# Routing of the first half moved into the last steps of the attention, at two places of a four-layer kernel

## The reference

```python
    def _L0_xattn_ref(q, k, v, mask, Wq, Wk, Wv, Wo):
        qh = split_heads(q, Wq, Sq)
        kh = split_heads(k, Wk, Sk)
        vh = split_heads(v, Wv, Sk)
        scores = jnp.einsum('bhqd,bhkd->bhqk', qh, kh) / jnp.sqrt(jnp.asarray(D_K, qh.dtype))
        m = mask[:, None, :, :]
        scores = jnp.where(m == 0, jnp.asarray(-1000000000.0, scores.dtype), scores)
        p = jax.nn.softmax(scores, axis=-1)
        out = jnp.einsum('bhqk,bhkd->bhqd', p, vh)
        out = out.transpose(0, 2, 1, 3).reshape(B, Sq, H * D_K)
        return out @ Wo.T

    def _L0_ffn_ref(x, gate_w, fc_w, proj_w):
        gates = jax.nn.softmax(xt @ gate_w, axis=-1)
        top_v, top_i = jax.lax.top_k(gates, K)
        top_v = top_v / jnp.sum(top_v, axis=-1, keepdims=True)
        h = jnp.einsum('nd,edf->enf', xt, fc_w)
        h = jax.nn.gelu(h, approximate=False)
        eo = jnp.einsum('enf,efd->end', h, proj_w)
        ...
        out = jnp.sum(sel * top_v[:, :, None], axis=1)

    x = x + _L0_xattn_ref(_layernorm(x, axis=-1), ctx_1024, ctx_1024, mask_Bx1xS2_if1, ...)
    x = x + _L0_ffn_ref(_layernorm(x, axis=-1), L0_ffn_gate_w, L0_ffn_fc_w, L0_ffn_proj_w)
    ...
    x = x + _L3_xattn_ref(_layernorm(x, axis=-1), ...)
    x = x + _L3_ffn_ref(_layernorm(x, axis=-1), ...)
```

## Time and profile before

| | us |
|---|---|
| three executions | 757.03, 757.04, 758.2 |
| median | 757.04 |
| profiled execution | 763.77 |
| its span, from the first to the last instruction | 762.0 |
| PE busy | 551.9 (72%) |
| DVE busy | 356.6 (47%) |
| POOL busy | 306.9 (40%) |
| ACT busy | 240.0 (31%) |
| chain that ended last, PE's share | 53% |
| chain that ended last, DVE's share | 19% |

### The profile page before, as it was taken

How to read it: one execution, slowest core, us unless ns; L and a number is a source line. 1 busy time by engine, 2 the same in 40 slices (tenths; PEclk the granted TensorE clock), 3 DMA queues, 4 the chain that set the end, 5 groups by cost and what they waited for, 6 DMA issues and landing times.

```text
span 762.0 us, 13194 instructions
## 1 busy us (share of the span) xinstructions
PE 551.9 (72%) x3830; PEld 472.1 (62%) x3845; DVE 356.6 (47%) x1306; ACT 240.0 (31%) x615; POOL 306.9 (40%) x415
## 2 busy tenths in 40 slices
PE   4998439999742535999864169959980599999930
PEld 2676319999632534989522147737770599999930
DVE  6788830001509745001249948887787022222232
ACT  1453005555310101655310023425420233333310
POOL 6000277648360162969450000000005777457634
PEclk9998559999955555999985569969965599999985
DMA  9930013324210010444110070030001122122222
GB/s 281 301 119 2 14 59 93 92 76 107 80 49 0 10 54 27 123 113 128 49 38 2 16 219 1 0 111 1 1 1 38 53 77 70 43 57 73 59 65 62
DMA packets 74485, 52.65 MB, mean 69 GB/s; under 512 B 9339, under 2 KB 67620, under 8 KB 74285
## 3 DMA queue, kind: packets, MB, share of 16 engines
q1 hardware_dynamic: 68301, 39.58, 18.0%
q0 software_dynamic: 6144, 12.60, 5.9%
HBM read 32.71 MB, written 19.43 MB: 68 GB/s over the span
## 4 chain that ended last, share of the span: by engine, by line
PE 53%; DVE 19%; issue 17%; another core or an unknown queue 4%; POOL 4%; DMA 2%; SPq 1%; ACT 1%; POOLq 0%; DVEq 0%; ACTq 0%
PE bank L1612 21%; PE bank L1626 14%; PE bank L1445 5%; PE bank L1600 2%; POOL XNR L553 2%; PE bank L1533 2%; PE bank L1502 2%; DVE XNR L804 2%; DVE stats L780 1%; POOL YG L553 1%; PE bank L1522 1%; PE bank L1565 1%; DVE X L1002 1%; DVE minus_half_vyy L798 1%
## 5 line engine op out<-in xcount | busy, mean ns | idle before, releaser
L539 POOL DMA_INDIRECT xs<-XNR,slot_i x96 | 94.2, 981 | 264.8 <-DVE slot_i L962 243.4
L1612 PE MATMUL bank<-xT,wcur 128*128 128x128 f32 x1288 | 179.7, 285 | 1.2 <-issue 0.4
L1612 PEld LDWEIGHTS bank<-xT,wcur 128*128 128x128 f32 x1288 | 164.3, 198 | 5.7 <-issue 2.1
L987 DVE TENSOR_TENSOR hT<-gb,bank 128x512 f32<-128x512 f32 x46 | 31.7, 688 | 109.0 <-ACT gb L647 109.0
L1002 DVE SCALAR_TENSOR_TENSOR X<-XNR,gates,X 128x128 f32<-128x128 f32 x48 | 14.3, 370 | 133.0 <-DMA XNR<-ys,slot_i 133.0
L571 POOL COPY wcur<-WA 128x512 f32 x92 | 56.4, 616 | 20.9 <-PE bank L1612 18.3
L553 POOL DMA_INDIRECT XNR<-ys,slot_i x48 | 47.1, 982 | 34.9 <-DMA ys<-Y 23.6
L1600 PE MATMUL bank<-ident,xrow 128*128 128x128 f32 x138 | 39.4, 289 | 26.4 <-DMA xrow<-xs 16.0
L647 ACT ACTIVATE hT<-bank 128x512 f32<-128x512 f32 (+1 forms) x92 | 45.1, 491 | 41.1 <-issue 16.4
L553 POOL DMA_INDIRECT YG<-ys,slot_i x48 | 48.1, 1001 | 11.1 <-issue 10.7
L655 ACT ACTIVATE Y<-bank 128x128 f32<-128x128 f32 x138 | 38.3, 278 | 42.2 <-PE bank L1626 30.5
(11 more groups left out here) (311 smaller groups left out, 1044.3 us busy)
## 6 DMA issues: line engine op xcount, KB each, us to landing
xrow<-xs SPq DMA_DIRECT2D x138, 64.0 KB
ys<-Y SPq DMA_DIRECT2D x138, 64.0 KB
WA<-in_fc_dram SPq DMA_DIRECT2D x16, 256.0 KB, 4.4
xs<-zeros SPq DMA_DIRECT2D x2, 1472.0 KB, 10.5
WA<-in_pj_dram SPq DMA_DIRECT2D x8, 256.0 KB, 6.0
WB<-in_fc_dram SPq DMA_DIRECT2D x8, 256.0 KB, 4.6
WB<-in_pj_dram SPq DMA_DIRECT2D x8, 256.0 KB, 6.6
xs<-XNR,slot_i POOLq DMA_INDIRECT x96
```

Of the source, the lines that this page charges most:

```text
L539: pool.indirect_dma_start(out=xs_dram[g], out_offset=bass.IndirectOffsetOnAxis(ap=slot_i[:, k, t:t + 1], axis=0), in_=XNR[:, t, :], in_off ...
L987: dve.tensor_tensor(hT[s][:, :, :], gb[s % 2][:, :, :], bank[2 + s % 2][:, :].rearrange("p (c t) -> p c t", c=4), ALU.mult).then_inc(ex_mu ...
L1612: ins = pe.matmul(dst, wcur[:, s4, at:at + P], xT[s4 % 2][:, :], start=True, stop=not L["bias"])
```

## The change

All of it concerns `attention` of layers 0 and 3 and the routing behind it.

- VectorE: aggregate and root of half 0 stand at the end of step 14 (EARLY_N), its scaling at step 15, its choices at step 19, ahead of the last X add. Its slots come right after the last step, then the norm of half 1, the shares of half 0 and the whole router of half 1.
- TensorE: the transposes of half 0 stand at the end of step 17 (EARLY_T) and go to banks 0 and 1, behind a wait for the last `s_sub`; its logits at the end of step 18; then the ranks of half 0, transposes and logits of half 1, ranks of half 1.
- ScalarE: the two copies of half 0's transposes stand at step 17, the exponentials of half 0's router ahead of the copies of half 1.
- GpSimd and SyncE have the same lists as before.

The diff, without the parts that only split `router` into `choices`, `places` and `shares`:

```diff
+EARLY_N, EARLY_T = TILES - 2, TILES + 1
...
         @block.scalar
...
-            def evac_xt(n, batches=range(B)):
+            def evac_xt(n, batches=range(B), first=4):
...
+                    if s == EARLY_T:
+                        evac_xt(n + 1, range(GB), 0)
...
-            attention(0)
-            evac_xt(1)
-            for g in range(GROUPS):
-                router(g)
+            attention(0, 0)
+            router(0)
+            evac_xt(1, range(GB, B))
+            router(1)
...
         @block.vector
...
-                    if s == TILES + 2:
+                    if s == EARLY_N:
                         ln_aggregate(half(0))
                         ln_rstd(GT)
+                    if s == EARLY_N + 1:
+                        ln_scale(half(0), XNR[:, 0:GT, :], xn_ready)
                     if s == TILES + 3:
-                        ln_scale(half(0), XNR[:, 0:GT, :], xn_ready)
+                        dve.wait_ge(const_ready, 2)
+                        choices(layer, 0)
                 link(ins)
+                places(layer, 0)
                 ln_aggregate(half(1), GT)
                 ln_rstd(GT)
                 ln_scale(half(1), XNR[:, GT:TILES, :], xn_ready)
+                shares(layer, 0)
+                router(layer, 1)
...
-            attention(0)
-            dve.wait_ge(const_ready, 2)
-            for g in range(GROUPS):
-                router(0, g)
+            attention(0, 0)
             setup1()
...
         @block.tensor
...
+                    if s == EARLY_T:
+                        pe.wait_ge(s_sub, (a + 1) * TILES)
+                        transposes(n + 1, range(GB), 0)
+                    if s == EARLY_T + 1:
+                        gate_logits(n + 1, 0, gate_w)
...
             def router(layer, n, gate_w):
-                for g in range(GROUPS):
-                    logits(n, g, gate_w)
-                for g in range(GROUPS):
-                    ranks(layer, g)
+                ranks(layer, 0)
+                logits(n, 1, gate_w)
+                ranks(layer, 1)
```

More of the change, by code:

```diff
@@ L600, in _ @@
         def _(act):
-            def evac_xt(n, batches=range(B)):
+            def evac_xt(n, batches=range(B), first=4):
                 for q in batches:
                     act.wait_ge(xt_mm, turn_of(n, q) + 1)
-                    act.activation(XT[:, q * BT:(q + 1) * BT, :], bank[4 + q][:, :].rearrange("p (t c) -> p t c", c=P),
+                    act.activation(XT[:, q * BT:(q + 1) * BT, :], bank[first + q][:, :].rearrange("p (t c) -> p t c", c=P),
                                    ACT.Copy).then_inc(xt_ready, 1)
@@ L611, in setup, with attention @@
                     act.activation(M[:, b, :], bank[1 + b % 2][:, :], ACT.Copy).then_inc(m_evac, 1)
-            def attention(a):
+            def attention(a, n):
                 for s in range(TILES + 4):
@@ L760, in _ @@
             evac_xt(4)
-            attention(1)
-            evac_xt(5)
-            for g in range(GROUPS):
-                router(2 * GROUPS + g)
+            attention(1, 4)
+            router(2 * GROUPS)
+            evac_xt(5, range(GB, B))
+            router(2 * GROUPS + 1)
             experts(2)
@@ L869, in values, with attention @@
                 ins.then_inc(setup_evac, 1)
-            def attention(a):
+            def attention(a, layer):
                 for s in range(TILES + 6):
@@ L909, in attention, with choices @@
                 ln_scale(half(1), XNR[:, GT:TILES, :], xn_ready)
-            def router(layer, g):
+                shares(layer, 0)
+                router(layer, 1)
+            def choices(layer, g):
                 r = layer * GROUPS + g
                 flat = [P, GT, E]
-                half_tiles = slice(g * GT, (g + 1) * GT)
                 dve.wait_ge(lg_mm, r + 1)
@@ L945, in router, with places @@
                 dve.tensor_tensor(de[:, :], m2[:, :], m1[:, :], ALU.subtract).then_inc(dl_ready, 1)
+            def places(layer, g):
+                r = layer * GROUPS + g
+                flat = [P, GT, E]
+                half_tiles = slice(g * GT, (g + 1) * GT)
                 dve.wait_ge(rank_mm, r + 1)
@@ L970, in router, with shares @@
                 dve.wait_ge(experts_known, r + 1)
+            def shares(layer, g):
+                r = layer * GROUPS + g
+                half_tiles = slice(g * GT, (g + 1) * GT)
                 dve.wait_ge(ex_ready, r + 1)
@@ L980, in router @@
                 link(dve.tensor_tensor(gates[:, 1, half_tiles], pr2[:, :], den[:, :], ALU.mult))
+            def router(layer, g):
+                choices(layer, g)
+                places(layer, g)
+                shares(layer, g)
             def products():
@@ L1271, in _ @@
             ffn2()
-            attention(1)
-            for g in range(GROUPS):
-                router(2, g)
+            attention(1, 2)
             products()
@@ L1481, in ffn2, with transposes @@
                         turn(2 * p - 1)
-            def transposes(n, batches=range(B)):
+            def transposes(n, batches=range(B), first=4):
                 for q in batches:
@@ L1487, in transposes, with attention @@
                         pe.wait_ge(xn_ready, turn_of(n, q) * BT + j + 1)
-                        ins = pe.transpose(bank[4 + q][:, j * P:(j + 1) * P], XNR[:, q * BT + j, :], ident[:, :])
+                        ins = pe.transpose(bank[first + q][:, j * P:(j + 1) * P], XNR[:, q * BT + j, :], ident[:, :])
                     ins.then_inc(xt_mm, 1)
-            def attention(a, n):
+            def attention(a, n, gate_w):
                 def tokens_out(q):
@@ L1662, in _ @@
             pe.wait_ge(mrow_ready, 1)
-            attention(0, 0)
+            attention(0, 0, gate0)
             router(0, 1, gate0)
@@ L1694, in _ @@
             pe.wait_ge(mrow_ready, 2)
-            attention(1, 4)
+            attention(1, 4, gate3)
             router(2, 5, gate3)
```

4 lines of the change are left out of this document (3 added, 1 removed).

## The result

The changed kernel is slower: 764.91 us median (764.6 to 765.01) against 757.37 (757.03 to 758.2) for the kernel before, ratio 1.0097, 95% interval 1.008 to 1.0115, or +7.5 us. The forecast was 757.6, and its range ended at 763.0. The profiled execution took 764.82, as long as the plain ones, while that of the kernel before took 763.77, 6.4 over its median. So the two spans, 762.0 and 763.1, differ by 1.1 us only, and the traces have to be compared stage by stage.

A forecast was written before the change was run, and what follows sets the result against it. The prediction took setup1 to bound the experts' start after attention 0 once changed, and the scatters after attention 3. It added +1.95 and -1.4 us, +0.55 on 757.04, for 757.6 us; range 754.2 to 763.0.

The forecast's parts named there:

- What bounds the places: After attention 0, setup1 becomes the bound, its late copies having hidden an undisturbed 112.1; after attention 3, the scatters bind.
- Attention's tail and the logits: After attention 0: tail 3.6 us later, half 0's norm 4.6 earlier; logits run 74.4 to 77.9, nothing won.
- D: Rival, faster: clock stays full some 3 us longer at attention's tail, slots 3.2 earlier; -3.0 us, 754.0, chance 0.15.
- Scatters: Half 0's scatters start 1.5 us earlier after attention 0 and 1.4 us earlier after attention 3.
- Half 1 later: After attention 0: half 1's choices start 5.8 us later, at 96.2; setup1 follows and experts start at 114.7.
- mechanism A: The forecast itself: setup1 becomes the bound after attention 0, the place after attention 3 gains; 757.6, chance 0.47.
- late releases at 0: The sum adds no time for late semaphore releases, after attention 0 or after attention 3.
- rival B: Slower: late releases hit VectorE's chain in the last third of 16 transfers; 3.6 us more after attention 0, 762.1, chance 0.2.
- Second place: After attention 3: scatters bind, no setup1 follows, and their earlier start gives -1.4 us.
- The cover of 1.2 us: After attention 3: half 1's expert numbers come at 593.7, scatters end at 594.9, leaving 1.2 us.
- C: Rival, slower: half 1's scaling stretches two scatters by 0.7 us each, cancelling the gain after attention 3; 759.0, chance 0.1.
- E: Rival, faster: setup1 doesn't bind, its products overlapping the routing, so both places gain; -2.9 us, 754.1, chance 0.08.

The follow-up runs named there:

- e3: Changed kernel with setup1 taken out of the line behind half 1's routing; ratio 1.0006 to the kernel before.
- e9: Kernel before, order untouched, with GpSimd pausing after eight transfers in layer 1's first-half scatters and layer 0's second-half gathers; ratio 1.0004.
- e11: Changed order at both places, with setup1 aside, early expert numbers and pauses in three runs of transfers; ratio 1.0000 or thereabouts: 0.9999 (0.9987 to 1.0011).
- e6: Changed kernel with setup1 aside, and weight copies and row turning started on half 0's expert numbers alone; ratio 1.0007 to the kernel before.
- e13: Changed kernel, unaltered, timed again on a chip where no trace shows late releases; ratio 1.0048 to the kernel before.
- e4: Changed kernel with only 8 of the 16 first-half scatters in layer 0, part of the computation missing; ratio 1.0078 to the kernel before.
- e7: Changed kernel with GpSimd waiting behind the eighth first-half scatter in layers 0 and 3 until eight have landed; ratio 1.0041 to the kernel before.
- e14: Kernel before with pauses in layer 1's scatters and layer 0's second gathers, on a chip without late releases; ratio 0.9999.
- e16: Changed kernel with a pause behind the eighth scatter in layers 0 and 3, on a chip without late releases; ratio 1.0048 to the kernel before.
- e10: Kernel before with pauses in layer 1's scatters and layer 0's second gathers, and setup1 aside too; ratio 1.0000.
- e18: Kernel before with pauses in layer 1's scatters and layer 0's second gathers, on a chip with late releases; ratio 0.9863.
- e15: Changed order with setup1 aside, early expert numbers and pauses in layer 1's scatters, layer 0's second gathers and layer 3's scatters; ratio 0.9996 to the kernel before.
- e17: Changed kernel, unaltered, timed again on a chip with late releases; ratio 1.0110 to the kernel before.
- e5: Changed kernel, unaltered, timed again beside three other versions on one chip; ratio 1.0115 to the kernel before, +8.7 us.

## Why the prediction was wrong

In short: what bounds the places was right. The term that failed is the lateness of releases, which the sum carried at nothing; with what came with it, it was 5.3 us at the first place, and it took back the gain of the second. The rest of the first place's term was sized a little small.

**What bounds the places.** Right. That setup1 becomes the bound of the first one is shown by e3 (110.25 behind the rows) and by the transpose right behind the copies in every trace of the changed kernel. That the late copy in the earlier trace rows hid an undisturbed 112.1 is shown by e9.

**Attention's tail and the logits.** Step 15 at 65.48 for 65.3 was right. The logits' end at 78 was met by luck, since two terms of it were wrong and made up for each other. In all twelve traces with the early order at the first place TensorE idles for 2.9 us behind step 14, and the granted clock falls to half at 66.1 to 68.8 us. (That the idle stretch brings it down is not shown.) The last norm of O then ends at 73.2 to 73.9, where 71.9 was laid out, and the logits begin at 75.4 to 76.0 instead of 74.4. In seven of the twelve the clock was back at full from 75.1 to 76.6, for 3.4 to 6.8 us: there the logits took 1.85 to 2.25 and the choices came at 77.4 to 78.1. In the other five it stayed half until 115.7 or later, the logits took 3.42, and the choices came at 79.0 to 79.5.

**D.** It had the clock stay full some 3 us longer. It fell earlier instead: at 66.1 to 68.8, where with the old order it falls at 69.5 to 72.7 (70.0 in the trace of the kernel before; the digit that the prediction calls slice 3 is the fourth of the row). What D promised, logits at full clock, came in seven traces by the clock's return, and brings the choices at most 0.7 ahead of the forecast; D had 1.7 (3.2 against the kernel before).

**Scatters.** The first was forecast at 87.1. It came at 88.03 on record, at 86.4 to 86.9 in six traces, 87.16 in e11, and at 88.0 to 90.2 in the others (90.2 in e6). Nothing late is in this term.

**Half 1 later.** With the late releases gone (e13, e4) every step of this term is within 0.8 us of the forecast. This is the half of the loss that I had as mechanism A: +2.1 to +3.8, where the sum carried +1.95. The term was undersized, apart from the clock, because I took the middle between 112.1 and 113.41 as the start to compare with. Where releases come in time, 112.1 is the only one.

**The term that failed: late releases at 0.** The sum has no lateness at either place. I gave rival B a chance of 0.2 since only two runs of the trace showed it and one didn't. It was the rest of the loss. Chain from the choices to kT 15.15 instead of 10.35: +4.8 at the first place (3.3 of late releases, 1.0 beside the weight copies, the rest single longer instructions); logits of half 1 released 0.55 late: +0.55; choices of half 1 without that lateness 1.2 after the forecast, from the clock. 114.7 + 4.8 + 0.55 + 1.2 = 121.2, seen 121.09. B priced this at +3.6 and came to 762.1 for the whole; the lateness was 1.8 more (4.8 + 0.55) and the clock 1.2. That the lateness is in plain executions too is shown by e7, whose pause gives back 5.5 us over both places.

**Second place.** -1.4 forecast. The 1.9 us at the scatters are there. The cover of 1.2 us that I had named was spent by a late release of 3.1 us on half 1's logits, which I hadn't priced since I looked for B only in VectorE's own links, and by five late links of half a microsecond behind it. Where releases come in time, e13 goes from the start of attention 3 (498.45) to the end of the span in 249.3, and e9 and e14 in 250.2 and 250.5: -0.8 to -1.1, near the forecast. The two places make +1.0 to +3.0 there, and the plain executions +3.6. The stretch between the places, from the first transpose to attention 3, isn't neutral either, as the prediction had it: 384.2 in e13 and 384.5 in e16 against 382.8 to 383.4 in e9, e10 and e14. And the profiled execution of e13 (749.5) was the fastest of its five. What lengthens that stretch wasn't resolved.

**C.** Two scatters beside half 1's scaling (91.4 to 93.5) took 1.07 and 0.97, against 0.97 alone; C had put 0.7 more on each. The rule of the Trainium skill that stood behind C (SBUF — State Buffer, Who interferes with whom: the two lock each other out of a port pair for whole instructions) costs the scatters 0.1 us at most for the short scalings here; the measurement decides.

**E.** Out, by e3 and every trace.

What stays open: what the late releases are, and why some chips or hours have them. That they hang on a long unbroken run of GpSimd transfers is shown by e4, e7 and e18 together; that the run must be 16 long, or what happens inside the chip, is not. Nor is such a run enough: in the trace of the kernel before, the one from 372 to 394 us shows no late release. e11 and e15 start the experts 1.3 and 0.1 us before 112.13, and have half 1's numbers in time, but aren't faster. The traces tell a part: e11 takes 0.8 us longer than e9 from there to attention 3 (383.57 against 382.76). At the second place its scatters start 1.46 earlier against attention 3, its pause costs 1.3 of that, and the first transpose comes only 0.2 earlier.

## What to carry to other kernels

An engine's chain that is moved under a long run of GpSimd's indirect transfers can lose more than it gains. Count the waits that come to lie in the second half of the run, and price them by this case: some 0.5 us, up to 1.2, for a linked instruction in the last third, and 0.6 to 9.7 us for products that end behind the eighth transfer. If a trace shows late releases at all, break the run with one wait for what is already in flight (it cost GpSimd 1.3 to 1.5 us) before anything is reordered: it gave more than any order here. And when a profiled execution is 6 us over the plain ones, ask which of its waits the other kernel's trace lacks before you subtract the two.

## What the runs showed of the hardware

- In unbroken runs of 16 indirect transfers, on some chips, releases of VectorE's own semaphores came 0.5 to 1.2 us late from the twelfth transfer on, and those of TensorE's products 0.6 to 9.7 us late from the eighth on (0.64 in the changed kernel, 8.3 in the kernel before, 9.0 in e17, 9.7 in e4, at the softmax of attention 1). Not every such run shows it. On two other chips no trace shows any (e9 to e16). The kernel before takes 757 to 762 us on the first kind and 747 to 748 on the second.
- A wait behind the eighth of the 16, which held the ninth back by 1.3 to 1.5 us, left no link late, and products at most 1.1 (e7, e18).
- With the early order the granted clock fell to half in the attention's tail in all twelve traces, at 66.1 to 68.8 us, and in seven it was full again for 3.4 to 6.8 us from 75.1 to 76.6 on; the logits of half 0 took 3.42 or 1.85 by it.
- VectorE's 0.17 us instructions took 0.48 to 0.53 beside GpSimd's copies of weights (110.9 to 112.5 in the changed kernel, 109.8 to 110.9 in e5).
